# Four column tiles of 32 in place of two of 64 in the spectral mix of a 2-D FFT block

## The chip, the cores and the metric

The kernel runs on one core of a Trainium2 chip. The metric is the device time of one execution in microseconds; the figure for a kernel is the median of its runs. A profile is of one execution. PE is TensorE's multiplication, PEld its weight load, DVE VectorE, ACT ScalarE, POOL GpSimd, SP SyncE.

## The reference

The input x is (8, 32, 32, 192) in f32. Layer 0 is a Fourier block, layer 1 a gated scan with an MLP. Only the first half of layer 0 matters here:

```python
xn = _layernorm(x, norm1_w, norm1_b)
xf = jnp.fft.rfft2(xn, axes=(1, 2), norm='ortho')        # (8, 32, 17, 192)
xf = xf.reshape(B, h, w // 2 + 1, NB, BS)                # NB = 8 blocks of BS = 24
o1 = jnp.einsum('bhwni,hwnio->bhwno', xf, w1c) + b1c     # complex, own weights for each (h, w, n)
o1 = jax.lax.complex(jax.nn.relu(o1.real), jax.nn.relu(o1.imag))
xs = jnp.fft.irfft2(o1.reshape(B, h, w // 2 + 1, C), s=(h, w), axes=(1, 2), norm='ortho')
...
return xs + residual + mlp_out
```

For each of 32 x 17 frequencies and each of 8 channel blocks, 8 images' 24 complex channels are multiplied by a complex 24 x 24 matrix. That is the spectral mix.

## The kernel before

`fourier` does layer 0 up to the transform over height. The transform over width has been stored in memory as `rows_spectrum`. The 17 width frequencies ("bins") are taken in groups of two, g = 0 to 7 (`NG` = 8), and one left over, the real bin 16, as group 8 (`bins = 1`). The channels are halved, s = 0 and 1, 96 each, that is four blocks (`NH` = 4). A unit u = 2g + s is one group and one half.

On PE, `columns` (line 642) transforms the next group over height: `d2` (two bins of all images, a single buffer) against the table `fwd_h`, 8 matmuls for a unit, into PSUM banks 4 and 5. DVE scales the result into `xh` (line 535). ACT's queue issues the `expand` DMAs (line 291), which spread `xh` into the block-diagonal operand `S[s]`: 96 rows of channels and 4 rows for the bias, 64 columns (real and imaginary part, 4 blocks, 8 images; `2 * NH * B` = 64), and 64 pairs of bin and height. For one bin and height the columns of `S` lie 64 elements apart.

`products` (line 667) multiplies: for each of 32 heights h and each bin k of the group, `S[s][:, :, k * H + h]`, 100 x 64, is the loaded operand and the weights `Wt[p][s][:, k, h, :]`, 100 x 48, the moving one. Bin 0 goes to PSUM partitions 0 to 63, bin 1 to 64 to 127. Eight heights fill a bank j; the last matmul of a bank raises `mixed`. The moving tile alternates between `Wt` and `row_bufs` (p = 0 and 1), so a line of the profile can name either.

ACT (`unit`, lines 449 and 451) copies the odd columns of a bank into `cross` with real and imaginary halves exchanged, four activations of 32 partitions a bank, DVE adds them (line 564, `summed`), transposes `Y`, applies the relu into `Z`, and PE's `inverse` (line 677) transforms back over height. DVE copies the result into `d3`, and POOL's queue stores it as `rows_mixed` (line 382). The last inverse, of the single bin, has 64 rows and 32 columns.

The order on PE for a group is written out: products of s = 0, columns of the next group's s = 0, inverse of the group before, products of s = 1, columns of the next group's s = 1. The first two groups and the last two are unrolled, the four between are two passes of a loop. A bank is written again only when `summed` of the unit before has passed.

SP's queue holds, for a group: wait for `mixed` of s = 0 and load the weights of group g + 2 for that s (lines 282 and 283, two bins), wait for `hdft` and load `d2` of group g + 2 (`spectrum_rows`, line 315), then the same weights for s = 1.

Of the kernel before, what the change touches and what calls it, by code (L numbers as in the profile page):

```python
# [14 lines left out]
B, H, W, C = 8, 32, 32, 192  # L15
# [8 lines left out]
NH = NB // 2  # L24
# [50 lines left out]
def passed(eng, sem, value):  # L75

    if not isinstance(value, int) or value > 0:
        eng.wait_ge(sem, value)
# [137 lines left out]
def fourier(nc, t, sh, F1, F2):  # L216

    X = sh.X
    with ExitStack() as ctx:
        def sb(name, shape, dt=F32):  # L220
            return ctx.enter_context(nc.sbuf_tensor(name, shape, dt))

        def sem(name):
# [20 lines left out]
        S = [sb(f"S{s}", [HALF + NH, 2 * NH * B, 2 * H]) for s in range(2)]  # L244

        Wt = [[sb(f"Wt{s}", [HALF + NH, 2, H, 2 * BS]) for s in range(2)],
              [row_bufs[s][0:HALF + NH].rearrange("p a t c -> p (a t c)").rearrange("p (k h c) -> p k h c", k=2, h=H)
               for s in range(2)]]
# [5 lines left out]
        ps = ctx.enter_context(nc.psum_tensor("psF", [P, 8, 512], F32))  # L254
# [355 lines left out]
        @block.tensor  # L610
        def _(pe):
            pe.wait_ge(row_table, 16)

            def rows(i, s):
                b = 2 * i + s
                for q in range(4):
                    pe.wait_ge(normed if q < 2 else normed_a, TPB // 2 * b + 2 * (q % 2) + 2)
                    if q == 0:
                        passed(pe, d1_done, 4 * (b - 1))
                    pe.matmul(ps[:, 4 * s + q, 0:2 * C], fwd_w[:, :],  # L620
                              xn[s][:, 2 * q:2 * q + 2, :].rearrange("p t c -> p (t c)"),
                              start=True, stop=True).then_inc(rows_done, 1)

            for s in range(2):
                rows(0, s)
            with pe.Fori(1, B // 2) as i:
                for s in range(2):
                    rows(i, s)

            def columns(u, s, g):  # L630

                if s == 0:
                    pe.wait_ge(d2_in, 16 * (g + 1))
                for q in range(2):
                    if isinstance(g, int) and g == 0:
                        table = fwd_h0[:, 0:4 * H]
                        passed(pe, k16_done, 7 * s)
                    else:
                        table = fwd_h[:, :]
                        pe.wait_ge(xh_done, 4 * (u - 1) + 2 * q + 2)  # L640
                    for b in range(4):
                        mm = pe.matmul(ps[0:HALF, 4 + q, P * b:P * b + P],  # L642
                                       d2[:, 4 * q + b, HALF * s:HALF * s + HALF], table, start=True, stop=True)
                    mm.then_inc(hdft, 1)


            pe.wait_ge(d1_done, 4 * B)
            pe.wait_ge(consts, 16 * N_CONST)
            for s in range(2):
                columns(s, s, 0)  # L650
                for b in range(B):
                    mm = pe.matmul(ps[0:HALF, 6 + s, 2 * H * b:2 * H * b + 2 * H],
                                   d2[:, b, HALF * s:HALF * s + HALF], fwd_h0[:, 4 * H:], start=True, stop=True)
                mm.then_inc(k16_dft, 1)

            def products(u, s, g, p, times, bins=2):

                pe.wait_ge(s_in[s], 16 * NH * (g + 1) if bins == 2 else 16 * NH * (NG + 2))
                pe.wait_ge(w_in[p][s], 64 * times if bins == 2 else 64 * (times - 1) + 32)
                if isinstance(g, int) and g == 0:  # L660
                    pe.wait_ge(ones_in, 32)
                for j in range(4):
                    passed(pe, summed, 4 * (u - 1) + j + 1)
                    for hl in range(8):
                        for k in range(bins):
                            h = 8 * j + hl
                            mm = pe.matmul(ps[2 * H * k:2 * H * k + 2 * H, j, 48 * hl:48 * hl + 48],  # L667
                                           S[s][:, :, k * H + h], Wt[p][s][:, k, h, :], start=True, stop=True)
                    mm.then_inc(mixed, 1)

            def inverse(g, rows=P, width=P):
                pe.wait_ge(relu, 2 * (g + 1))
                z = Z[0:rows].rearrange("p b s c -> p (b s c)")
                for j in range(4):

                    passed(pe, d3_done, 4 * g + j - 1)
                    pe.matmul(ps[0:width, 6 + j % 2, 0:384], inv_h[0:rows, 0:width], z[:, 384 * j:384 * j + 384],
                              start=True, stop=True).then_inc(inv_done, 1)

            def group(g, p, times):  # L680
                for s in range(2):
                    products(2 * g + s, s, g, p, times)
                    if not (isinstance(g, int) and g == NG - 1):
                        columns(2 * (g + 1) + s, s, g + 1)
                    if s == 0 and not (isinstance(g, int) and g == 0):
                        inverse(g - 1)


            pe.wait_ge(k16_done, 13)
            for g in range(2):  # L690
                group(g, g, 1)
            with pe.Fori(1, NG // 2 - 1) as gg:
                for p in range(2):
                    group(2 * gg + p, p, gg + 1)
            for g in range(NG - 2, NG):
                group(g, g % 2, NG // 2)
            inverse(NG - 1)
            for s in range(2):
                products(2 * NG + s, s, NG, 0, NG // 2 + 1, 1)
            inverse(NG, 2 * H, H)  # L700
# [954 lines left out]
```

## Time and profile before

| What | Value |
|---|---|
| median of 3 runs | 1285.8 us (1284.46 to 1286.18) |
| the profiled execution | 1284.34 us |
| its span | 1282.9 us, mean granted clock 0.891 |
| PE, weight load busy | 1122.5 us (87%), 903.4 us (70%) |
| DVE, ACT, POOL busy | 884.2, 665.6, 347.0 us |
| line 667, records of each kind | 2176, from 116.6 to 339.8 us |

The span runs from the first to the last instruction; 1.4 us of the execution lie around it. The page has the span in 40 slices of 32 us; the stage of the change is in slices 4 to 11. The records of multiplications overlap, since each holds its latency too: the spacing of starts, and not the length of a record, is the rate.

### The profile page before, as it was taken

The numbers are of one execution on the slowest core, as the hardware profiler recorded it, in microseconds if no ns is written. First come the engines' busy times: TensorE is split into PE (matmuls) and PEld (weight loads), VectorE is DVE, ScalarE is ACT, GpSimd is POOL, SyncE is SP. The second block draws the span as 40 slices with busy tenths as digits, with TensorE's granted clock in tenths as the row PEclk, the third lists the DMA queues.
The fourth block names the chain that finished last, engine by engine and source line by source line (L and its number), as shares of the span: only waits on it lengthen the run. The fifth ranks groups of instructions, "written<-read, shape, count | busy, mean of one in ns | idle before, by whom it ended". The sixth has DMA issues, their size and how long they took to land. (4 is left out here: it accounts for less than half of the span.)

```text
span 1282.9 us, 22505 instructions
## 1 busy us (share of the span) xinstructions
PE 1122.5 (87%) x7072; PEld 903.4 (70%) x7072; DVE 884.2 (69%) x2183; ACT 665.6 (52%) x1299; POOL 347.0 (27%) x350
## 2 busy tenths in 40 slices
PE   2535799998754899999979999999999879999998
PEld 1225799887532788888965766767766668889997
DVE  6626456465447788877776867959969867766665
ACT  2421343434133555766656756756654346676655
POOL 4564010011017100000012843724716611111110
PEclk8765677777566899999989999999999979999999
DMA  8644999994180000000010000000000000001001
GB/s 248 148 123 86 185 176 199 195 184 102 33 239 21 1 1 0 0 0 0 0 43 1 1 1 1 1 1 1 1 1 1 1 1 25 25 25 37 25 25 37
DMA packets 153073, 70.22 MB, mean 55 GB/s; under 512 B 117968, under 2 KB 145392, under 8 KB 153008
## 3 DMA queue, kind: packets, MB, share of 16 engines
q1 hardware_dynamic: 129208, 47.38, 18.1%
q10 hardware_dynamic: 19232, 9.18, 3.7%
q0 software_dynamic: 4576, 12.93, 3.5%
q8 instruction: 33, 0.54, 0.2%
q14 instruction: 24, 0.20, 0.1%
HBM read 43.91 MB, written 18.87 MB: 49 GB/s over the span
## 5 line engine op out<-in xcount | busy, mean ns | idle before, releaser
L1128 PE MATMUL L_conv_ps<-w2hl,L_conv_hhi 128*128 128x384 f32 x768 | 229.2, 366 | 1.3 <-DVE X L1024 1.3
L938 ACT ACTIVATE L_conv_hf<-L_conv_ps,L_conv_b 128x512 f32<-128x512 f32 x192 | 132.2, 688 | 176.4 <-PE L_conv_ps L1109 171.9
L1128 PE MATMUL L_conv_ps<-w2hl,L_conv_hlo 128*128 128x192 f32 x768 | 188.7, 252 | 0.0
L1014 DVE TENSOR_TENSOR L_conv_hlo<-L_conv_hf,L_conv_hhi 128x512 fp32r<-128x512 f32 x192 | 129.4, 688 | 85.5 <-ACT L_conv_hhi L947 82.9
L1520 PE MATMUL sc_ps<-sc_hi,wh 128*128 128x512 f32 (+1 forms) x440 | 161.6, 439 | 3.3 <-ACT sc_prod L1302 3.2
L1128 PEld LDWEIGHTS L_conv_ps<-w2hl,L_conv_hhi 128*128 128x128 f32 x768 | 144.8, 189 | 4.8 <-DVE X L1024 2.1
L1520 PE MATMUL sc_ps<-sc_hi,wl 128*128 128x512 f32 (+1 forms) x440 | 147.8, 393 | 0.0
L1128 PEld LDWEIGHTS L_conv_ps<-w2hl,L_conv_hlo 128*128 128x128 f32 x768 | 146.7, 192 | 0.0
L449 ACT ACTIVATE cross<-psF 32x192 f32<-32x192 f32 x136 | 43.9, 323 | 174.4 <-PE psF L667 159.3
L1375 DVE TENSOR_TENSOR sc_prod<-sc_ps,sc_gate 128x512 f32<-128x512 f32 x168 | 110.2, 680 | 14.9 <-PE sc_ps L1520 14.8
L947 ACT ACTIVATE L_conv_hhi<-L_conv_hf 128x512 fp32r<-128x512 f32 x192 | 116.2, 622 | 0.0
L1520 PEld LDWEIGHTS sc_ps<-sc_hi,wh 128*128 128x128 f32 (+1 forms) x440 | 70.5, 186 | 57.5 <-issue 43.0
L1520 PE MATMUL sc_ps<-sc_lo,wh 128*128 128x512 f32 (+1 forms) x440 | 108.8, 394 | 0.0
L1242 POOL TENSOR_TENSOR sc_lo<-sc_prod,sc_hi 128x512 fp32r<-128x512 f32 x64 | 95.3, 1512 | 22.7 <-ACT sc_hi L1318 22.7
L899 POOL TENSOR_TENSOR X<-X,L_conv_b 128x192 f32 x64 | 36.7, 605 | 194.4 <-DVE L_conv_xn L998 194.4
L642 PE MATMUL psF<-fwd_h,d 128*96 128x128 f32 x256 | 56.0, 409 | 37.0 <-DVE dc L552 19.7
L564 DVE TENSOR_TENSOR Y<-psF,cross 128x192 f32<-128x192 f32 (+1 forms) x72 | 25.6, 356 | 87.4 <-ACT cross L451 87.4
L1109 PE MATMUL L_conv_ps<-L_conv_thi,w1h 128*128 128x512 f32 x192 | 78.3, 408 | 6.7 <-ACT L_conv_hf L938 3.9
L1520 PEld LDWEIGHTS sc_ps<-sc_lo,wh 128*128 128x128 f32 (+1 forms) x440 | 70.5, 188 | 17.5 <-issue 2.9
L1109 PE MATMUL L_conv_ps<-L_conv_tst,w1h 128*128 128x512 f32 x192 | 77.5, 404 | 2.5 <-DVE L_conv_tst L1009 2.5
L642 PEld LDWEIGHTS psF<-fwd_h,d 128*96 128x96 f32 x256 | 51.6, 269 | 39.0 <-DVE dc L552 19.8
L1520 PEld LDWEIGHTS sc_ps<-sc_hi,wl 128*128 128x128 f32 (+1 forms) x440 | 70.8, 188 | 9.9
(138 smaller groups left out, 2321.8 us busy)
## 6 DMA issues: line engine op xcount, KB each, us to landing
row_bufs<-in_L_conv_w SPq DMA_DIRECT2D x16, 576.0 KB
Wt<-in_L_conv_w SPq DMA_DIRECT2D x14, 576.0 KB
X<-in_x POOLq DMA_DIRECT2D x8, 768.0 KB, 6.1
rows_spectrum<-row_bufs SPq DMA_DIRECT2D x32, 192.0 KB, 3.4
d<-rows_spectrum SPq DMA_DIRECT2D x8, 768.0 KB, 5.0
S<-xh ACTq DMA_DIRECT2D x64, 96.0 KB
rows_mixed<-d POOLq DMA_DIRECT2D x32, 192.0 KB, 6.0
d<-rows_mixed SPq DMA_DIRECT2D x8, 768.0 KB, 9.5
```

The lines of the kernel that those rows point to most:

```text
L449: nc.scalar.activation(cross[j % 2][re:re + H], v[im:im + H, :, :, 1], ACT.Copy, scale=-1.0).then_inc(crossed, 1)
L564: nc.vector.tensor_tensor(Y[0:n, 8 * j:8 * j + 8, :], v[0:n, :, :, 0], cross[j % 2][0:n], ALU.add).then_inc(summed, 1)
L642: mm = pe.matmul(ps[0:HALF, 4 + q, P * b:P * b + P], d2[:, 4 * q + b, HALF * s:HALF * s + HALF], table, start=True, stop=True)
L899: nc.gpsimd.tensor_tensor(X[:, GT * i + k, :], X[:, GT * i + k, :], b2[:, :], ALU.add).then_inc(biased, 1)
L938: nc.scalar.activation(hf[:, m % 3, :], ps[:, RB + m % 2, :], gelu, bias=b1[:, m:m + 1]).then_inc(act1, 1)
L947: nc.scalar.activation(hhi[:, m, :], hf[:, m % 3, :], ACT.Copy).then_inc(h_hi, 1)
L1014: nc.vector.tensor_tensor(hlo[:, m, :], hf[:, m % 3, :], hhi[:, m, :].bitcast(F32), ALU.subtract).then_inc(h_lo, 1)
L1109: mm = pe.matmul(ps[:, RB + m % 2, :], w, x[:, :], start=(q == 0), stop=(q == 4))
L1128: mm = pe.matmul(o, x, w, start=(m == 0 and n == 0), stop=(m == MT - 1 and n == 1), skip_group_check=True)
L1242: nc.gpsimd.tensor_tensor(lo[c][:, j, :], value(c, s)[:, j, :], hi[c][:, j, :].bitcast(F32), ALU.subtract).then_inc(q["h_lo"], 1)
L1375: step_product = nc.vector.tensor_tensor(prod[c][:, j, :], ps[:, 3 * c + j, :], gate[c][:, j, :], ALU.mult)
L1520: return pe.matmul(out, ww[rows, cols], x[rows, j, :], start=first, stop=last, skip_group_check=True)
```

## The change

Each matmul of `products` is split in two by the loaded operand's columns: r = 0 takes the 32 of the real part, r = 1 the 32 of the imaginary part, both with the same moving operand. The output of bin k and part r goes to PSUM partitions from (2k + r) x 32. The values and where they lie in PSUM are as before.

```diff
                     for hl in range(8):
-                        for k in range(bins):
-                            h = 8 * j + hl
-                            mm = pe.matmul(ps[2 * H * k:2 * H * k + 2 * H, j, 48 * hl:48 * hl + 48],
-                                           S[s][:, :, k * H + h], Wt[p][s][:, k, h, :], start=True, stop=True)
+                        for k, r in itertools.product(range(bins), range(2)):
+                            h, at = 8 * j + hl, (2 * k + r) * NH * B
+                            mm = pe.matmul(ps[at:at + NH * B, j, 48 * hl:48 * hl + 48],
+                                           S[s][:, NH * B * r:NH * B * (r + 1), k * H + h], Wt[p][s][:, k, h, :],
+                                           start=True, stop=True)
                     mm.then_inc(mixed, 1)
```

## Rows read from the trace of the kernel before

**Rows 1.** The page: busy time, slices of 32 us, DMA queues.

```profile
PE 1122.5 (87%) x7072; PEld 903.4 (70%) x7072; DVE 884.2 (69%) x2183; ACT 665.6 (52%) x1299; POOL 347.0 (27%) x350
...
PE   2535799998754899999979999999999879999998
...
PEclk8765677777566899999989999999999979999999
DMA  8644999994180000000010000000000000001001
...
q8 instruction: 33, 0.54, 0.2%
q14 instruction: 24, 0.20, 0.1%
```

**Rows 2.** Stretches of 16 us: busy us (records), PEclk, DMA share, GB/s.

```profile
176.00:192.00 16.00, 15.64 (x186) 13.78 (x186) 8.65 (x16) 8.53 (x28) 3.03 (x4) 0.71 1.15 170
224.00:240.00 16.00, 14.79 (x188) 13.00 (x188) 8.85 (x16) 7.66 (x24) 2.74 (x4) 0.89 1.17 195
256.00:272.00 16.00, 15.80 (x175) 13.60 (x173) 10.00 (x20) 5.30 (x17) 3.02 (x4) 0.75 1.06 176
```

**Rows 3.** Timeline of PE, 110 to 345 us: start, length.

```profile
114.11 1.49 PE L652 MATMUL psF<-fwd_h,d 128*96 128x64 f32 x16
...
138.19 7.37 PE L667 MATMUL psF<-row_bufs,S 100*64 100x48 f32 x128
152.20 3.73 PE L642 MATMUL psF<-fwd_h,d 128*96 128x128 f32 x16 [6.64 <-DMA d<-rows_spectrum]
...
206.52 1.46 PE L677 MATMUL psF<-Z,inv_h 128*128 128x384 f32 x4
...
245.84 7.37 PE L667 MATMUL psF<-row_bufs,S 100*64 100x48 f32 x128
253.14 3.73 PE L642 MATMUL psF<-fwd_h,d 128*96 128x128 f32 x16
...
325.75 14.39 PE L667 MATMUL psF<-Wt,S 100*64 100x48 f32 x128
344.26 1.48 PE L677 MATMUL psF<-Z,inv_h 64*32 64x384 f32 x2 [4.12 <-DVE Z L575]
```

**Rows 4.** Stretches, line 667 alone: PE, PEld busy us (records), PEclk.

```profile
160.00:167.20 7.20, 7.20 (x128) 7.19 (x128) 0.86 1.18 211
196.10:203.30 7.20, 7.20 (x128) 7.19 (x128) 0.72 0.88 206
285.40:292.60 7.20, 7.20 (x128) 7.15 (x128) 0.92 1.16 209
325.75:327.50 1.75, 1.75 (x16) 1.75 (x17) 1.00 0.00 0
336.40:338.10 1.70, 1.70 (x18) 1.70 (x17) 0.50 0.00 0
```

**Rows 5.** Line 677, all of it, then from 343 us: ns min/median/max.

```profile
L677 PE MATMUL psF<-Z,inv_h x72: 486/488/1009, 155.7 to 348.7; 128*128 128x384 f32 x64, 64*32 64x384 f32 x8
...
L677 PEld LDWEIGHTS psF<-Z,inv_h x8: 122/160/173, 344.3 to 348.1; 64*32 64x32 f32 x8
L677 PE MATMUL psF<-Z,inv_h x8: 844/844/844, 344.3 to 348.7; 64*32 64x384 f32 x8
```

**Rows 6.** Lines 652 and 667 (here 325 to 340 us): ns min/median/max.

```profile
L652 PEld LDWEIGHTS psF<-fwd_h,d x32: 163/165/284, 88.8 to 115.3; 128*96 128x96 f32 x32
...
L667 PEld LDWEIGHTS psF<-Wt,S x128: 185/203/207, 325.7 to 339.8; 100*64 100x64 f32 x128
```

**Rows 7.** A stretch of 30 ns, line 667 alone: PE, PEld busy (records).

```profile
260.12:260.15 0.03, 0.02 (x2) 0.02 (x2) 1.00 0.97 60
```

**Rows 8.** Line 640, 251.9 to 252.4 us: PE's sequencer.

```profile
L640 PEldq FUSED_REGOPS  x1: 60/60/60, 252.0 to 252.0; - x1
L640 PEldq ALU_OP  x1: 32/32/32, 252.4 to 252.4; - x1
```

**Rows 9.** Timeline of SP's queue: start, length of the issue.

```profile
127.89 0.47 SPq L282 DMA_DIRECT2D row_bufs<-in_L_conv_w  x1
...
132.08 5.84 SPq L283 DMA_DIRECT2D row_bufs<-in_L_conv_b  x1
...
141.49 4.81 SPq L283 DMA_DIRECT2D Wt<-in_L_conv_b  x1
146.35 0.80 SPq L315 DMA_DIRECT2D d<-rows_spectrum  x1
...
246.08 0.35 SPq L315 DMA_DIRECT2D d<-rows_spectrum  x1
```

**Rows 10.** The page's DMA issues: KB, us to landing.

```profile
d<-rows_spectrum SPq DMA_DIRECT2D x8, 768.0 KB, 5.0
```

**Rows 11.** Timeline of ACT in one unit.

```profile
275.84 0.32 ACT L449 ACTIVATE cross<-psF 32x192 f32<-32x192 f32 x1 [6.94 <-PE psF L667]
276.19 0.32 ACT L451 ACTIVATE cross<-psF 32x192 f32<-32x192 f32 x1
```

## The prediction

> **What bounds the kernel now.** I read the page first. PE is busy 87% of the span, and it is at or near full between 112 and 340 us, the stage with line 667, while the granted clock there is mixed and the DMA share is at its highest [rows 1]. Stretches of that stage say the same: PE 14.8 to 15.8 us busy of 16, against 8.7 to 10.0 on DVE and 5.3 to 8.5 on ACT; the DMA share is over 1 [rows 2]. So time taken from PE here can reach the end, unless a transfer holds it.
>
> The timeline of PE gives the beat of the stage [rows 3]. One unit of line 667 is 64 calls of `pe.matmul` and leaves 128 records of multiplication and 128 of weight load: each f32 call is two loads and two multiplications, four instructions. A unit lasts 7.37 us with its last record's 0.28 us, so the records start (7.37 - 0.28) / 127 = 55.8 ns apart. There are 16 such units, and two more with one bin, which stand together as x128 in 14.39 us: (14.39 - 0.28) / 127 = 111.1 ns apart. In these two, all outputs go to one column tile; in the 16, two tiles alternate. The spacing is exactly double with half the tiles. So the tiles work beside each other, each with a cycle of 111 ns for a load and a multiplication, and neither unit is bound by how fast instructions come.
>
> What fills 111 ns? It isn't the granted clock: units at 0.72, 0.86 and 0.92 each show 128 records in 7.2 us, and the one-tile units keep their pace from clock 1.00 to 0.50 [rows 4]. A multiplication costs two clocks for a column: two of 384 columns at the low level start 1.48 - 0.84 = 0.64 us apart, and four at the high level (1.46 - 0.49) / 3 = 0.32 us [rows 3, 5]. For 48 columns that is 40 ns at 2.4 GHz and 80 at 1.2, both under 111, so it is hidden behind something of fixed speed, the load. A load's record is 163 ns for 96 columns of `d2`, 185 for 64 of `S` in a tile, and 122 for 32 columns in the last inverse [rows 5, 6], the shortest of each. The 96-column ones repeat every (1.49 - 0.25) / 15 = 83 ns [rows 3], so some 80 of the 163 are latency; that leaves about 105 for 64 columns in a tile and about 42 for 32. I read the tile's cycle as 64 columns x 1.67 ns + 4.
>
> The Trainium skill (TensorE: Matmul & The Clock Gate, section "LDWEIGHTS (loading the stationary operand)") gives a load as its columns / 1.2 ns. The 83 ns of 96 columns agree (80); the 111 ns of a tile of 64 (53) don't, unless load and multiplication are serial. By that rule on a single path for all loads, the sum of columns stays the same and the time with it.
>
> **The change, part by part.** Removed: nothing of the arithmetic. Each call of 64 columns becomes two of 32, with the same moving operand. A unit goes from 256 to 512 PE instructions, the two last units together from 256 to 512. No wait, no semaphore count, no DMA and no instruction of another engine is touched: `mixed` is raised by the last call of j as before.
>
> (a) Per tile. A load of 32 columns would be 32 x 1.67 = 53 ns, the cycle about 58 at the high level; at the low one the multiplication's 80 is longer, about 85. With four tiles beside each other the records start 14.5 to 21 ns apart. From above: if the cycle stays at 111, 27.8 ns; if all loads share one path of 0.83 ns a column (from the 83 ns of 96), 26.7 + 2.5 = 29.2.
>
> (b) Per instruction. Four tiles need two instructions in each such spacing. The start itself is no bound: between 260.12 and 260.15 us, where a unit begins, two loads and two multiplications have started [rows 7]. How fast the sequencer can bring instructions, no row shows directly. It is at least one in 27.9 ns (55.8 / 2). A better bound: its own register instructions at line 640 stand at 252.0 and 252.4 us with q = 0's four calls between them, 16 instructions; less the 60 ns of the first, that is at most about 21 ns each [rows 8]. Line 667 executes meanwhile and keeps the queue full, so the true value lies below. Bounds: 7.2 (it never binds) and 21 ns. I take the geometric middle, 12 ns, so 24 ns a record, because nothing stands nearer to either end.
>
> (c) The sum. A unit: 256 x 24 = 6.15 us in place of 128 x 55.8 = 7.15, 1.0 us less. The first three units give nothing: PE stands idle 6.64 us for `d<-rows_spectrum` before 152.20 [rows 3], and SP issues that load only at 146.35, behind its own weight loads, whose issues take up to 5.84 us each from 127.9 us on [rows 9]. They don't wait for PE there. So 13 x 1.0 = 13.0 us. The two last units have two tiles in place of one and mostly the low clock: 85 / 2 = 42.5 ns, 256 x 42.5 = 10.9 against 128 x 111.1 = 14.2, 3.3 us less. In all 16.3.
>
> (d) What is late next. `d2` is a single buffer: SP issues its load at 246.08, after the columns before it, its median from issue to landing is 5.0 us, and PE wants it at 253.14, after a unit [rows 3, 9, 10]. That leaves 253.14 - 251.1 = 2.1 us in each first unit of a group: more than 1.0, so it holds nothing at my value, and caps the gain at 2.1 there. ACT needs 16 x 0.345 = 5.5 us for a unit's `cross` [rows 11], less than 6.15 and beside the columns anyway. A program twice as long in this stage is fetched from memory; the instruction queues moved 0.3% of the engines' span in all [rows 1], so I cost that at nothing, and a stall at the loop's one back edge at up to 3 us for the range.
>
> The profiled execution is 1284.3 us around a span of 1282.9; the median shown is 1285.8, 1.5 above. 1284.3 - 16.3 + 1.5 = 1269.5, rounded to 1269.
>
> **The rivals.** *Cap*: instructions come freely (under 8 ns). Units fall to 3.7 us (high clock) or 5.4 (low), `d2` limits every first unit to 2.1, its gain in the second is about 2.5: 7 x 2.5 + 6 x 2.1 + 3.3 = 33 us, so 1252. For it: four instructions start within 30 ns [rows 7]. Against it: a 7 ns supply would have to come through a sequencer that shows no instruction of its own shorter than 32 ns [rows 8].
>
> *Supply*: the sequencer needs more than 14.0 ns for an instruction (7.15 us / 512), and PE waits for it instead of for its tiles. This is the one that ends on the other side. At 17.5 ns a unit is 8.96 us, 1.8 longer; the wait before 152 us swallows the first three; 13 x 1.8 - 3.3 = +20, so 1306. At 21 ns: 10.75, 3.6 longer, 13 x 3.6 + (10.8 - 6.6) - 3.4 = +48, so 1333. For it: at 27.9 ns an instruction, today's stream is the densest that this trace shows. Against it: the tight pairs and a queue that refills while it drains.
>
> *Nothing changes*: a tile's cycle stays 111 ns whatever its columns (27.8 ns a record, 7.12 us a unit, two last units 55.6 and as before), 1286; or the shared path: 29.2, a unit 7.48, 13 x 0.33 = +4.3, the last two 256 x 42.5 as above, -3.3, so 1287. Against it: the 122 ns of a 32-column load [rows 6].
>
> A fixed price for each multiplication speaks against small tiles. The Trainium skill (TensorEngine Tiling (Array Packing), section "Performance Considerations", "Instruction Overhead") says that each matmul has about 60 cycles of overhead and that one shouldn't take a tiling factor from a dimension that is already small; 48 moving columns are. At 2.4 GHz that is an estimate of 25 ns a record, 256 x 25 = 6.4 us a unit, 9.8 us saved in 13; at 1.2 GHz 50 ns, 12.8 us a unit and some 80 us lost. Two multiplications within 30 ns [rows 7] don't show such a price across tiles. The chance of *supply* covers it.
>
> **How the numbers follow.** My forecast (supply 8 to 13 ns) 0.42, *cap* 0.14, *nothing changes* 0.15, *supply* 0.29. The likeliest case's own range is 1256 to 1281. The range must cross to *supply*: 1250 to 1310 leaves out some 0.04 below and 0.13 above. 0.2% is 2.6 us, about what a measurement of this kernel can tell from no change. So faster 0.42 + 0.14 = 0.56, same 0.15, slower 0.29.
>
> **What would show it.** Line 667 doubles to 4352 records of each kind, 100x32. A unit between 5 and 7 us, x256, shows (a) and (b); loads of about 130 ns show the halved load. If the unit is over 7.2 us and its length doesn't depend on the granted clock, the supply binds; if it is 7.1, the tile's cycle didn't shrink. The last two units tell (a) from (b), since two tiles ask for half the supply: near 3.7 to 5.4 us each if the cycle shrinks. A wait of PE for `d<-rows_spectrum` in every group shows the cap. The wait before 152 us should grow by what the first three units save. What would make the number wrong is the 12 ns, which is a middle and not a reading.

## The result and the profile after

The changed kernel takes 1301.39 us, the median of 4 runs (1300.02 to 1304.95), against 1285.13 of 4 runs of the kernel before (1280.43 to 1286.18): a ratio of 1.0143, 95% interval 1.0115 to 1.017. It is slower, where 1269 and a gain were forecast. The profiled execution took 1300.29 us, its span is 1298.9, and the mean granted clock rose from 0.891 to 0.909.

The page of the changed kernel, lines that answer to [rows 1]:

```profile
PE 1081.6 (83%) x9248; PEld 859.8 (66%) x9248; DVE 889.5 (68%) x2183; ACT 666.9 (51%) x1299; POOL 345.1 (27%) x350
...
PE   2534667578745699999988999999999879999998
...
q8 instruction: 57, 0.93, 0.3%
```

PE is busy 41 us less, in a span that is 16 us longer. Its digits in slices 4 to 11 (counted from 0) fell from 7, 9, 9, 9, 9, 8, 7, 5 to 6, 6, 7, 5, 7, 8, 7, 4. The other engines are busy within 1% of before. Of the queues' rows one changed plainly in its number of packets: 57 instruction packets on queue q8 in place of 33, about 16 KB each.

The groups of PE's instructions in the stage show what stands in the holes. The kernel before, 110 to 356 us (records, busy us, mean ns, idle before and what ended it):

```profile
L667 PE MATMUL psF<-Wt,S 100*64 100x48 f32 x1152 | 73.3, 292 | 1.0 <-DVE x L549 1.0
L667 PE MATMUL psF<-row_bufs,S 100*64 100x48 f32 x1024 | 59.0, 290 | 0.0
L642 PE MATMUL psF<-fwd_h,d 128*96 128x128 f32 x240 | 52.3, 408 | 26.3 <-DVE dc L552 19.7 <-DMA d<-rows_spectrum 6.6
```

The changed kernel, 110 to 372 us:

```profile
L667 PE MATMUL psF<-Wt,S 100*32 100x48 f32 x2304 | 53.7, 250 | 30.5 <-issue 29.5 <-DVE x L549 1.0
L642 PE MATMUL psF<-fwd_h,d 128*96 128x128 f32 x240 | 49.0, 386 | 27.6 <-DVE dc L552 19.8 <-DMA d<-rows_spectrum 7.4 <-issue 0.4
L667 PE MATMUL psF<-row_bufs,S 100*32 100x48 f32 x2048 | 44.7, 252 | 25.5 <-issue 23.2 <-DMA S<-xh 2.1
```

Line 667 is busy 53.7 + 44.7 = 98.4 us in place of 132.3, 33.9 less: the multiplications themselves went faster than forecast. But PE stands idle 29.5 + 23.2 = 52.7 us within them, where it was 0, and the wait ends with "issue": for nothing that a semaphore shows. With 2.1 us of waiting for `S`, 0.8 more for `d2`, 1.1 more around the inverse, and 2.9 less in the columns, the stage should be 52.7 - 33.9 + 2.1 + 0.8 + 1.1 - 2.9 = 19.9 us longer. It is about 20: the last inverse starts at 365.27, 21.0 us later than in [rows 3], and the stage began 1.0 later. The next stages give some of it back, and the span is 16.0 longer.

The timeline of PE shows how the holes lie (the changed kernel; start, length, records, idle before):

```profile
188.13 2.95 PE L667 MATMUL psF<-Wt,S 100*32 100x48 f32 x141
194.26 2.63 PE L667 MATMUL psF<-Wt,S 100*32 100x48 f32 x115 [3.19 <-issue]
...
254.36 2.93 PE L667 MATMUL psF<-Wt,S 100*32 100x48 f32 x141
259.52 2.35 PE L667 MATMUL psF<-Wt,S 100*32 100x48 f32 x115 [2.23 <-issue]
261.80 1.55 PE L642 MATMUL psF<-fwd_h,d 128*96 128x128 f32 x12
263.74 0.68 PE L642 MATMUL psF<-fwd_h,d 128*96 128x128 f32 x4 [0.39 <-issue]
264.35 2.61 PE L667 MATMUL psF<-row_bufs,S 100*32 100x48 f32 x122
267.48 2.71 PE L667 MATMUL psF<-row_bufs,S 100*32 100x48 f32 x128 [0.52 <-issue]
272.94 0.41 PE L667 MATMUL psF<-row_bufs,S 100*32 100x48 f32 x6 [2.75 <-issue]
...
284.15 2.65 PE L667 MATMUL psF<-row_bufs,S 100*32 100x48 f32 x127 [1.40 <-issue]
291.05 1.01 PE L667 MATMUL psF<-row_bufs,S 100*32 100x48 f32 x35 [4.25 <-issue]
...
333.76 5.51 PE L667 MATMUL psF<-row_bufs,S 100*32 100x48 f32 x256
...
350.55 9.81 PE L667 MATMUL psF<-Wt,S 100*32 100x48 f32 x256
```

There are four things to see. Between gaps the records stand (2.71 - 0.24) / 127 = 19.4 ns apart, better than the forecast 24; a unit without a gap lasts 5.51 us, (5.51 - 0.24) / 255 = 20.7 ns. A unit with gaps lasts as long as its gaps make it, 272.94 + 0.41 - 264.35 = 9.0 us. And the gaps come at even distances: 115 + 12 of line 642 = 127 records, 4 + 122 = 126, 128, 127. Each record stands for one multiplication and one load, so a gap comes every 256 PE instructions. An instruction packet of 16 KB would hold 256 instructions of 64 bytes. And the gaps belong to places in the code: the lines from 188.13 and from 254.36 us are the same instructions in the loop's first and second pass, and both have the gap after record 141. The next two units break in the same way in both passes, after records 122 and 250 and after records 94 and 221.

The DMA view of two stretches of the changed kernel, about the gaps 257.29 to 259.52 and 270.19 to 272.94 (packets, MB, share of 16 engines), first 256.6 to 258.3 us:

```profile
q10 hardware_dynamic: 105, 0.16, 57.1%
...
q8 instruction: 1, 0.02, 5.4%
```

and 270.1 to 271.6 us:

```profile
q1 hardware_dynamic: 1079, 0.21, 122.8%
q10 hardware_dynamic: 14, 0.02, 8.8%
q8 instruction: 1, 0.02, 4.9%
```

In each stands one packet of q8, none stands in the 0.6 to 1.4 us before and after it, and PE resumes 1.2 to 1.4 us after the end of the stretch. In the second the packet stands among 1079 small ones of the weights.

### The profile page after: what moved, and what is told of

Same layout as the page of the kernel before. It is cut to its first block and busy times, and to the rows that moved or that the text cites. A ratio compares the mean times of both kernels' runs of the same rounds, so it can differ in the third digit from the quotient of the medians.

```text
span 1298.9 us, 26857 instructions
## 1 busy us (share of the span) xinstructions
PE 1081.6 (83%) x9248; PEld 859.8 (66%) x9248; DVE 889.5 (68%) x2183; ACT 666.9 (51%) x1299; POOL 345.1 (27%) x350
## 3 DMA queue, kind: packets, MB, share of 16 engines
q1 hardware_dynamic: 129208, 47.38, 18.4%
## 5 line engine op out<-in xcount | busy, mean ns | idle before, releaser
L449 ACT ACTIVATE cross<-psF 32x192 f32<-32x192 f32 x136 | 44.7, 328 | 193.3 <-PE psF L667 133.7
L642 PE MATMUL psF<-fwd_h,d 128*96 128x128 f32 x256 | 52.7, 389 | 38.0 <-DVE dc L552 19.8
L382 POOL DMA_DIRECT2D rows_mixed<-d x31 | 19.8, 641 | 223.8 <-DVE d L584 222.6
L667 PE MATMUL psF<-Wt,S 100*32 100x48 f32 x2304 | 53.7, 250 | 30.5 <-issue 29.5
```

The source lines that it names most:

```text
L449: nc.scalar.activation(cross[j % 2][re:re + H], v[im:im + H, :, :, 1], ACT.Copy, scale=-1.0).then_inc(crossed, 1)
L642: mm = pe.matmul(ps[0:HALF, 4 + q, P * b:P * b + P], d2[:, 4 * q + b, HALF * s:HALF * s + HALF], table, start=True, stop=True)
L667: mm = pe.matmul(ps[at:at + NH * B, j, 48 * hl:48 * hl + 48], S[s][:, NH * B * r:NH * B * (r + 1), k * H + h], Wt[p][s][:, k, h, :], start ...
```

## The experiments

The theory at the start (*fetch*): PE runs out of instructions because the next block of 256 must first come from memory; what counts is how long a block lasts. Its rivals: a steady rate (*supply*), and a cost of the 32-column tiles themselves. The ratios are against the kernel before on the same chip. Edits are against the changed kernel where nothing else is said.

**1. Only the two last units split** (the stretch where the DMA is nearly quiet).

```diff
+                    parts = 2 if bins == 1 else 1
-                        for k, r in itertools.product(range(bins), range(2)):
-                            h, at = 8 * j + hl, (2 * k + r) * NH * B
+                        for k, r in itertools.product(range(bins), range(parts)):
+                            n = 2 * NH * B // parts
+                            h, at = 8 * j + hl, 2 * H * k + n * r
```

> Four tiles only in the two last units (one bin, so two tiles of 32 in place of one of 64), the 16 others as before. Fetch theory (PE stands still because a block of 256 instructions is used up in 2.3 us and the next one isn't there yet): the last two units run as in the changed kernel, 9.8 us together in place of 14.4, without a stall, since their instructions still last 4.9 us a block and DMA is quiet there; 1285.1 - 4.6 = 1280.5 us. Tile theory (the small tiles themselves stall PE, wherever they are used): stalls of 2 to 5 us show in these units too and the time is 1285 or more.

1280.06 us (12 runs) against 1284.66 (17), ratio 0.9962 (0.9943 to 0.9981). The timeline of this kernel has the two units in one piece:

```profile
328.39 9.84 PE L669 MATMUL psF<-Wt,S 100*32 100x48 f32 x256
```

14.39 us became 9.84, 4.55 less, and the kernel gained 4.6, as the fetch theory had expected. In this stretch the small tiles cost nothing, and nothing takes the gain back.

**2 and 3. The weight loads cut from group 2 on, in the changed kernel and in the kernel before.** Both leave out 31 of 32 heights of each later weight load, so those units multiply with weights of an earlier group; the number of DMAs, semaphores and PE instructions stays.

```diff
-        def load_weights(eng, g, p, s, bins=2):
+        def load_weights(eng, g, p, s, bins=2, rows=H):
...
-                eng.dma_start(Wt[p][s][0:HALF, k], w_v[s, 2 * g + k]).then_inc(w_in[p][s], 16)
+                eng.dma_start(Wt[p][s][0:HALF, k, 0:rows], w_v[s, 2 * g + k][:, 0:rows]).then_inc(w_in[p][s], 16)
...
-                        load_weights(sp, g + 2, p, s)
+                        load_weights(sp, g + 2, p, s, 2, 1)
```

> The changed kernel with the weight loads from group 2 on cut to 1 of 32 heights (the other heights keep the weights of groups 0 and 1, so the mix is computed with stale weights there). Fetch theory: instruction blocks no longer queue behind the weight packets, so the stalls inside units shrink from 2 to 5 us to under 1.5 us each after 150 us, and most units last 5 to 6.5 us; the stage ends some 25 to 40 us earlier than in the changed kernel. Tile theory: units keep their stalls, and the stage ends less than 10 us earlier.

> The kernel before with the same cut weight loads (stale weights), to price the lighter DMA load by itself. Both theories: PE is full in this stage and doesn't wait for weights, so units stay at 7.15 us and only the 6.6 us wait for d before 152 us shrinks; 1278 to 1285 us.

The changed kernel with light loads took 1272.3 us, the kernel before with the same 1277.33. These are single runs, and the 17 runs of the kernel before alone spread over 7.6 us, so the times don't show by themselves that the sign turns. The traces agree with it: the last inverse starts at 334.88 in the first and at 338.89 in the second, from stages that began within 0.2 us of each other. The first one's stage ends 30 us before that of the changed kernel, within the 25 to 40 expected. Most of its gaps are shorter (not all: 3.46 before 216.70 was 1.72), and they stand in the same places:

```profile
206.28 2.64 PE L667 MATMUL psF<-row_bufs,S 100*32 100x48 f32 x127 [0.45 <-issue]
210.43 0.89 PE L667 MATMUL psF<-row_bufs,S 100*32 100x48 f32 x35 [1.51 <-issue]
...
216.70 1.11 PE L667 MATMUL psF<-Wt,S 100*32 100x48 f32 x44 [3.46 <-issue]
220.84 2.80 PE L667 MATMUL psF<-Wt,S 100*32 100x48 f32 x127 [3.03 <-issue]
224.81 2.00 PE L667 MATMUL psF<-Wt,S 100*32 100x48 f32 x85 [1.17 <-issue]
```

Issue gaps of line 667 sum to 19.6 + 12.4 = 32.0 us in place of 52.7. So some 21 us of them go with the weight packets, and 32 stay without them. Under 1.5 us each was expected after 150 us, and five are over 2.5, two of them over 3: that part of the expectation missed. From the start of a full block to the start of the next it takes 210.43 - 206.28 = 4.15 and 224.81 - 220.84 = 3.97 us here, and 4.0 to 5.5 over all four of them, but 4.7 to 7.0 in the changed kernel (272.94 - 267.48 = 5.46, 291.05 - 284.15 = 6.90). A block of split records lasts 2.7 to 2.8 us. A block of the kernel before lasts 128 x 55.8 ns = 7.1 us, which is longer than all of these, and that kernel has no gap. With the light loads it took 1277.33 us where 1278 to 1285 were expected, for the 6.64 us of waiting for `d2` before 152 us [rows 3] went as a whole.

**4. A filler beside the old tiles.** The kernel before, with one more matmul of 1 x 1 ahead of each call, so that the number of PE instructions is that of the changed kernel.

```diff
                         for k in range(bins):
                             h = 8 * j + hl
+                            pe.matmul(ps[2 * H * k:2 * H * k + 1, j, 400:401],
+                                      S[s][:, 0:1, k * H + h], Wt[p][s][:, k, h, 0:1], start=True, stop=True)
```

> The kernel before, tiles of 64 as they were, with a matmul of one column by one column put ahead of each call of line 667 in the same tile, into an unused PSUM column: 512 PE instructions a unit as in the changed kernel, without its tiles of 32. Fetch theory: a block lasts 3.6 to 4.5 us, so gaps put down to issue appear inside units, once a block, shorter than in the changed kernel, and the unit takes more than the 7.2 to 9 us of its own work. Tile theory: units of 7.2 to 9 us without gaps.

1690.57 us (2 runs), ratio 1.3157 (1.3118 to 1.3196): both expectations missed. Its timeline:

```profile
119.40 0.19 PE L667 MATMUL psF<-Wt,S 100*1 100x1 f32 x2 [0.97 <-DVE x L549]
119.52 0.42 PE L669 MATMUL psF<-Wt,S 100*64 100x48 f32 x2
119.86 0.19 PE L667 MATMUL psF<-Wt,S 100*1 100x1 f32 x2
119.98 0.42 PE L669 MATMUL psF<-Wt,S 100*64 100x48 f32 x2
```

The records of a call no longer overlap those of the next: a call takes 0.47 us in place of 0.11. The kernel is 406 us longer for 1088 calls, 0.37 us a call, each of which changes from one tile size to the other and back. So it doesn't measure the supply and says nothing of the dispute. That the change of size is the cause is argued, since no run varies it alone. Experiment 6 speaks for it: its units have one change within them, from two tiles to four, and last 7.00 us where 96 x 55.8 ns + 64 x 19.0 ns + 0.24 = 6.81 are to be expected, an estimate of 0.2 us for the change. A filler should have the tile of its neighbours.

**5. The split in half of the units** (s = 0 and the two last).

```diff
+                    parts = 2 if bins == 1 or s == 0 else 1
```

> Four tiles in the units of s = 0 (and in the two last ones), two in those of s = 1. The loop's body falls to some 1700 instructions, 108 KB. Fetch theory: if the instruction buffer keeps that, as it kept the body of before in its second pass, the loop's second pass shows no instruction packets and its two s = 0 units run without a gap in 4.5 to 5.5 us, while s = 0 units outside the loop and in its first pass, under the same load of other transfers, have gaps of 2 to 4 us. Tile theory: gaps in both passes alike.

1293.62 us (3 runs), ratio 1.0078 (1.0051 to 1.0105). The timeline of line 667 here (669 in this kernel), with units of both kinds:

```profile
179.34 1.98 PE L669 MATMUL psF<-Wt,S 100*32 100x48 f32 x85 [2.89 <-issue]
187.35 7.37 PE L669 MATMUL psF<-Wt,S 100*64 100x48 f32 x128
...
233.50 2.81 PE L669 MATMUL psF<-Wt,S 100*32 100x48 f32 x127 [5.61 <-issue]
...
247.37 7.36 PE L669 MATMUL psF<-Wt,S 100*64 100x48 f32 x128
```

The gaps stand in the split units alone. They stand in both passes of the loop: the fetch theory had expected the second pass to be free of gaps and of instruction packets, so its expectation missed, and gaps in both passes are what the tile theory had expected. Queue q8 settles it: the loop's second pass fetches its instructions again. Counting 64 bytes for each multiplication and load, the body of two groups (four units) is about 76 KB in the kernel before, 108 here and 141 in the changed kernel (PE's own register and wait instructions come on top, an estimated 4%). In the view of the DMA queues from 220 to 270 us, in the second pass, the kernel before has no row of q8 at all; the changed kernel has, from 218 to 270 us,

```profile
q8 instruction: 10, 0.16, 1.6%
```

and this one 9 packets from 215 to 265. So a body of 76 KB isn't fetched again, and one of 108 is.

**6 to 8. The split in one bank of four, or in two.** A bank is 8 of a unit's 32 heights; in these kernels split records are mixed among slow ones, and the loop's body has about 92 KB (bank 3) or 108 KB (two banks). The two last units are split in all.

```diff
+                    parts = 2 if bins == 1 or j == 3 else 1           # 6: bank 3
+                    parts = 2 if bins == 1 or j in (0, 3) else 1      # 7: banks 0 and 3
+                    parts = 2 if bins == 1 or j > 1 else 1            # 8: banks 2 and 3
```

> Four tiles in the last bank (j = 3) of each unit and in the two last units, two tiles elsewhere: 320 PE instructions a unit, and any 256 in a row last 4.7 us or more. Fetch theory: next to no gap, each bank 1.78 - 1.17 = 0.6 us shorter less some 0.2 for one more change of tile size; 13 x 0.4 + 4.6 = 10 us faster than before, 1275. Tile theory: a gap in each split bank, slower than the kernel with the last units alone (1280).

> Four tiles in banks j = 0 and 3, which stand on both sides of the slow columns matmuls, and in the two last units: 384 PE instructions a unit, any 256 in a row still last about 4.7 us. Fetch theory: short gaps at most, 0.8 to 0.9 us less a unit, 13 x 0.85 + 4.6 = 16 us faster than before, 1269. Tile theory: twice the gaps of the kernel with j = 3 alone, slower than 1280.

> The same number of instructions as with banks 0 and 3, but the split banks are 2 and 3, side by side: 256 instructions in 2.3 us, as dense as in the changed kernel, with one change of tile size less. Fetch theory: gaps of 1 to 3 us wherever a block ends within or just behind them, so slower than banks 0 and 3 by 5 to 20 us although PE has less to do. Tile theory, or a price for each instruction: the same time as banks 0 and 3 or 2 to 3 us less.

Bank 3: 1276.26 us (7 runs), ratio 0.9953 (0.9935 to 0.9971), where 1275 was expected, and not one issue gap in line 669, inside the loop or outside. Banks 0 and 3: 1282.26 (12 runs), ratio 1.0000 (0.9983 to 1.0017), where 1269 was expected. Banks 2 and 3: 1283.62 (10 runs), ratio 0.9998 (0.9979 to 1.0016). The two last were expected 5 to 20 us apart and aren't told apart by their times. Both expectations of the fetch theory missed. Queue q8 from 215 to 265 us, bank 3 alone:

```profile
q8 instruction: 1, 0.02, 0.1%
```

and banks 0 and 3:

```profile
q8 instruction: 9, 0.15, 1.5%
```

The timeline at the loop's back edge, banks 0 and 3:

```profile
226.51 1.20 PE L669 MATMUL psF<-Wt,S 100*32 100x48 f32 x44 [3.88 <-issue]
233.38 5.90 PE L669 MATMUL psF<-Wt,S 100*32 100x48 f32 x148 [5.67 <-issue]
```

and the same place with bank 3 alone:

```profile
220.09 6.99 PE L669 MATMUL psF<-Wt,S 100*64 100x48 f32 x160
```

So the body of 92 KB stays, that of 108 doesn't, and the jump back into a body that has to be fetched costs 3.88 + 5.67 = 9.6 us in two gaps. That is most of the 13.0 us of gaps of this kernel, which take most of the 15.4 us that its line 669 is busy less than before. With banks 2 and 3 the gaps sum to 14.9 us: 2.42 + 3.87 = 6.3 at the back edge, and five of 1.2 to 2.7 elsewhere, where the kernel with banks 0 and 3 has four of 0.4 to 1.6. So split banks side by side do have the longer gaps away from the back edge, as the fetch theory says, but only by 5 us in all, and its back edge was 3.3 us shorter.

**9. A version within both limits.** Bank 3 everywhere; bank 0 too where the code isn't the loop's; all banks of unit 15, where few transfers run (the 5.51 us unit above); the two last units.

```diff
+                    parts = 2 if (bins == 1 or j == 3 or (j == 0 and isinstance(g, int))
+                                  or (isinstance(u, int) and u == 15)) else 1
```

> Bank 3 of every unit with four tiles, bank 0 too outside the loop, all banks of the last full unit (u = 15), and the two last units. The loop's body stays at the size (92 KB) that was not fetched again in its second pass. Fetch theory: no long gap; against the kernel with bank 3 alone 6 more split banks that count at 0.4 us and 1.5 us in unit 15, so 2 to 4 us faster, 1273. Tile theory: gaps with each split bank, slower than bank 3 alone.

1272.28 us (6 runs, 1269.15 to 1276.1) against 1283.52 (10), ratio 0.9916 (0.9887 to 0.9944). The groups of line 669 (667 before), 110 to 372 us:

```profile
L669 PE MATMUL psF<-Wt,S 100*32 100x48 f32 (+1 forms) x1664 | 64.5, 265 | 1.5 <-DVE x L549 1.0 <-issue 0.5
L669 PE MATMUL psF<-row_bufs,S 100*32 100x48 f32 (+1 forms) x1472 | 53.7, 269 | 2.1 <-DMA S<-xh 1.2 <-issue 0.9
```

Busy 14.1 us less than before and 1.4 us of issue gaps. It beats both kernels, and 1273 was expected. Its first two units with their columns, 416 records, ran from 117.44 to 133.16 without a gap while the weight loads ran too: 4.8 us for 256 PE instructions.

**10 and 11. The full split in a body that stays.** Four tiles in every unit, no weight loads for groups 2 to 7, and the loop's four groups read the weights of group 0, the two behind it those of groups 0 and 1: the output is of stale weights. The loop's body is one group (about 73 KB with PE's own register and wait instructions, four passes) in the one and two groups (about 147 KB, two passes) in the other; all else is equal.

```diff
-            with pe.Fori(1, NG // 2 - 1) as gg:
-                for p in range(2):
-                    group(2 * gg + p, p, gg + 1)
+            with pe.Fori(2, NG - 2) as g:                 # 10: one group in the body
+                group(g, 0, 1)
+            with pe.Fori(1, NG // 2 - 1) as gg:           # 11: two groups in the body
+                for p in range(2):
+                    group(2 * gg + p, 0, 1)
```

> Four tiles everywhere, as in the changed kernel, but no weights are loaded for groups 2 to 7 and the loop's four groups all read the weights of group 0 (so the mix of groups 2 to 7 uses stale weights). The loop on PE is then one group long (some 1150 instructions, 73 KB) and has four passes. Fetch theory: gaps in its first pass, none in the passes 2 to 4 and no instruction packets there; six units of 256 records of 4.5 to 5.5 us in a row. Tile theory: gaps in all passes.

> The same as the kernel with a loop of one group, the same tiles, the same transfers and the same stale weights, but the loop's body is two groups long (147 KB) and has two passes, as in the changed kernel. Fetch theory: instruction packets and gaps of 0.3 to 3 us in both passes, the stage 6 to 15 us longer than with the one-group body. Tile theory: the two kernels take the same time within 2 us.

1264.93 us against 1270.98, 6 us apart at the same number of executed matmuls. With one run each that is little by itself; the traces carry the argument. The timeline of the one-group body in its passes 2 to 4:

```profile
205.43 5.15 PE L664 MATMUL psF<-Wt,S 100*32 100x48 f32 x256
210.51 1.99 PE L639 MATMUL psF<-fwd_h,d 128*96 128x128 f32 x16
212.43 5.08 PE L664 MATMUL psF<-Wt,S 100*32 100x48 f32 x256
...
219.27 1.46 PE L675 MATMUL psF<-Z,inv_h 128*128 128x384 f32 x4
226.65 2.93 PE L675 MATMUL psF<-Z,inv_h 128*128 128x384 f32 x4 [5.93 <-DVE d L581]
229.51 5.16 PE L664 MATMUL psF<-Wt,S 100*32 100x48 f32 x256
```

and the two-group body over the same time:

```profile
206.25 2.65 PE L664 MATMUL psF<-Wt,S 100*32 100x48 f32 x127 [0.74 <-issue]
210.95 0.89 PE L664 MATMUL psF<-Wt,S 100*32 100x48 f32 x35 [2.05 <-issue]
...
217.57 1.19 PE L664 MATMUL psF<-Wt,S 100*32 100x48 f32 x44 [3.81 <-issue]
221.44 2.80 PE L664 MATMUL psF<-Wt,S 100*32 100x48 f32 x127 [2.68 <-issue]
```

With the body kept, 256 records stand in 5.07 to 5.16 us, (5.08 - 0.24) / 255 = 19.0 ns apart, with no gap, unit after unit. So neither the tiles nor a steady rate of the sequencer limits at 9.5 ns an instruction. From 165 to 250 us q8 has 4 packets in the one and 17 in the other; from 190 to 258 us, passes 2 to 4 of the one-group body, it has none in the one and 13 in the other. Issue gaps of line 664: 12.9 us, all outside passes 2 to 4, against 32.7. Within the loop they are 3.0 us, all in its first pass, against 18.4 in both passes. The rest stands in code that is the same in both, and differs there by 4.4 us from one execution to the other. The stage is 5.2 us longer with the two-group body, where 6 to 15 were expected. The difference is smaller than the 19.8 us of the gaps, because in the first kernel PE next waits for DVE's copy of the inverse (32.0 us in the whole stage, 11.1 in the second): that is the bound which stands behind the gaps.

## Why the prediction was wrong

**The step that failed** is in (d): "A program twice as long in this stage is fetched from memory; the instruction queues moved 0.3% of the engines' span in all [rows 1], so I cost that at nothing, and a stall at the loop's one back edge at up to 3 us for the range." The term put at nothing measured 52.7 us of gaps in line 667. The share was read rightly and said nothing: q8 went from 0.2% to 0.3%. It is a volume, and the cost hangs on how soon one packet is there against the time that its 256 instructions last. [Rows 3] had the second number, 128 x 55.8 ns = 7.1 us; the split brings it to 2.4 to 2.8. For the first number the changed kernel's full blocks give 4.7 to 7.0 us beside the weight loads, and those of experiments 2 and 11 3.4 to 5.5 without them; no row of before could show it, since there the fetch never came late. The second part of the step, the loop, was also wrong in size: both of its passes are fetched, and the back edge cost 1.72 + 5.22 us of gaps in the changed kernel, 9.6 in experiment 7, not 3.

**(a), per tile: right in direction, off in size.** The cycle of a 32-column tile was forecast at 58 ns at the high clock and 85 at the low. It is 4 x 19.0 = 76 with four tiles (experiment 10) and 2 x (9.81 - 0.28) / 255 = 75 with two, at a granted clock of 1.00 throughout. At 0.50 the 127 records from 238.75 us stand 19.8 ns apart, a cycle of 79. The Trainium skill (TensorE: Matmul & The Clock Gate, section "LDWEIGHTS (loading the stationary operand)") gives 32 / 1.2 = 27 ns for such a load; the trace shows half the columns taking a cycle from 111 to 75, so about 1.1 ns a column and 39 ns on top, and that rule alone doesn't give a tile's cycle. The two last units were forecast at 10.9 us and took 9.81: 4.6 us saved, not 3.3. That this came near is luck: 10.9 was the figure for the low clock, but they ran at 1.00 from end to end, for which 58 ns would have given 256 x 29 ns = 7.4 us.

**(b), per instruction: the value was too high, and it wasn't the term that decides.** 12 ns were taken within 7.2 and 21; at most 9.5 is shown. The range was honest, but both of its ends were a steady rate. Units forecast at 6.15 us take 5.1 to 5.5 where no block is late.

**(c), the sum:** line 667 was busy 33.9 us less over all its units, for which the forecast's own figures give 16 x 1.0 + 3.3 = 19.3; what of it the end would have seen without gaps isn't shown, since experiment 10 finds the next wait close behind. The wait before 152 us in [rows 3] did grow, from 6.64 to 7.38 us, but little, since the first three units had gaps of their own.

**The rivals.** *Supply* had the sign and nearly the time (1306 for 17.5 ns an instruction), by another mechanism: a unit of four tiles runs at 9.5 to 10.4 ns an instruction wherever no block is late (333.76 us after, experiment 10), which a sequencer of 14 ns or more can't. *Cap* is undecided in its condition, since at most 9.5 ns is shown and not under 8, and it fell in its price: no unit comes near 3.7 us, and experiment 10 shows a wait for a copy by DVE behind the gaps, not the wait for `d2`. *Nothing changes* fell with 19 to 20.7 ns a record. Of the Trainium skill's rule of some 60 cycles a matmul (TensorEngine Tiling (Array Packing), section "Instruction Overhead"), an estimate of 25 ns a record: the trace shows 19.0 across four tiles, less than that, and at the low clock no doubling. The kernel did become slower, but by the gaps and not by such a price.

**What is shown and what is argued.** Shown: gaps every 256 instructions, at the same places of the code in both passes, with a packet of q8 just ahead of two of them; fewer microseconds of gaps with fewer weight packets; in the same four-tile code, neither gaps nor packets of q8 where the body stays (passes 2 to 4 of experiment 10), and both where it doesn't (11); the limit of the body between 92 and 108 KB. Argued: that q8 is PE's instruction queue and a packet's 16 KB are the 256 instructions, which fits the distances and the count. Also argued: the 21 us that experiment 2 saves in gaps come with all that lighter loads change, so the traffic's part is known only as that sum. Open: when the fetch of a block is asked for, and so which part of the 4.7 to 7.0 us is its own and which is queueing; why the gaps of one kernel differ from 0.5 to 5.2 us; and how many blocks are held ahead, since experiment 9 ran at 4.8 us a block beside the weight loads without a gap, below the 7.0 that some blocks of the changed kernel took.

## What to carry to other kernels

Before splitting matmuls, multiply the time between two PE instructions by 256. Here most blocks that lasted 2.4 to 2.8 us were followed by an "issue" gap, and blocks of 4.8 us on average (the start of experiment 9) by none, with the weight loads beside both; where the limit lies between them isn't shown. Instructions repeated by a loop body that stays (here 92 KB or less) had no gap at 2.4 us a block. Split the stretches that are diluted by longer instructions or where the DMA is quiet, and look at the instruction queue's packets in the loop's later passes, none being the sign that the body is kept. The share of that queue says nothing of its latency.

## What the runs showed of the hardware

- Instruction packets of some 16 KB (57 packets, 0.93 MB); where blocks of 2.7 to 2.8 us were late, 4.7 to 7.0 us from the start of a full block to the start of the next beside the weight loads, 3.4 to 5.5 us without them (experiments 2 and 11).
- A loop body of about 92 KB wasn't fetched again in its second pass (1 packet), bodies of about 108 and 141 KB were (9 and 10 packets), and the jump back into them cost 6.3 to 9.6 us in two gaps.
- PE took one instruction in 9.5 ns for 512 instructions on end (a unit of 256 records of each kind, experiment 10).
- A 1-column call ahead of each 64-column call cost 0.37 us a pair, 406 us over 1088 calls.
- A load with its multiplication in a column tile: 111 ns for 64 columns, 75 to 79 for 32, nearly the same at both levels of the clock.
